# Running sum in fp32r, a shorter streamed router, and the position product moved from VectorE to GpSimd

## The reference

```python
h = _L0_tok_ref(x, W, b)             # path signature of depth 4, then a linear map
h = h + _L0_attn_ref(_layernorm(h), ...)
h = h + _L0_ffn_ref(_layernorm(h), ...)
h = h + _L1_attn_ref(_layernorm(h), ...)   # 8 heads of 16, relative positions
h = h + _L1_ffn_ref(_layernorm(h), ...)    # 64 experts, top 2, 256 places each
# fourth stage
attn1 = einsum('bhqd,bhkd->bhqk', rq, rk)
attn2 = einsum('bhqd,qkd->bhqk', rq, rel_k[idx])
attn = softmax((attn1 + attn2) / sqrt(c))
out = einsum('bhqk,bhkd->bhqd', attn, rv) + einsum('bhqk,qkd->bhqd', attn, rel_v[idx])
# router of the fifth
scores = sigmoid(xf @ gate_w.T); top_scores, top_idx = top_k(scores, 2)
top_scores = top_scores / (top_scores.sum(-1) + 1e-20) * 2.5
pos = cumulative count of the token's expert in the order of tokens - 1
buf[e, pos] = x of the pair, dropped where pos >= 256
```

## Time and profile before

| | us |
|---|---|
| median of 3 runs | 2156.07 (2155.49 to 2164.38) |
| the profiled execution, its own time | 2159.81 |
| its span | 2158.0 |
| signature stage | 0 to 568 |
| second and third stage | 568 to 984 |
| fourth stage, head | 984 to 1023 |
| fourth stage, batches | 1023 to 1811 |
| drain of the router | 1811 to 1888 |
| fifth stage and end | 1888 to 2158 |

### The profile page before, as it was taken

The page is one execution under the profiler, slowest core; times in us unless marked ns, Lnnn a source line. Parts: engine busy times, 40 slices in busy tenths (PEclk is TensorE's granted clock), DMA queues, the critical chain, the costliest instruction groups (busy, mean ns, idle before and its releaser), DMA issues. The chain is left out here.

```text
span 2158.0 us, 59101 instructions
## 1 busy us (share of the span) xinstructions
PE 1747.0 (81%) x21991; PEld 1432.7 (66%) x21991; DVE 1411.1 (65%) x3365; ACT 926.8 (43%) x2288; POOL 848.8 (39%) x1748
## 2 busy tenths in 40 slices
PE   5999999999789739943999999999998996066660
PEld 4888888888577639942887777777777775033440
DVE  6777777777578746655677777777777775123334
ACT  2111111111376407732677666666666663022220
POOL 3333333333016556631012433434444445655551
PEclk9999999999899859975999999999999998588875
DMA  8900000000300012230233333333333332064427
GB/s 309 103 0 0 0 0 0 0 0 0 135 28 26 26 52 70 72 107 25 53 62 71 69 66 67 71 67 70 72 74 76 71 69 45 33 191 123 125 66 242
DMA packets 312522, 147.59 MB, mean 68 GB/s; under 512 B 205094, under 2 KB 291140, under 8 KB 311876
## 3 DMA queue, kind: packets, MB, share of 16 engines
q1 hardware_dynamic: 299732, 118.38, 23.8%
q0 software_dynamic: 12544, 25.91, 3.7%
HBM read 72.03 MB, written 73.37 MB: 67 GB/s over the span
## 5 line engine op out<-in xcount | busy, mean ns | idle before, releaser
L1808 ACT ACTIVATE rel_e<-rel_s_ps,rel_neg_max 128x255 f32<-128x255 f32 x512 | 199.9, 476 | 68.9 <-DVE rel_neg_max L2082 68.4
L495 PE MATMUL tok_main_ps<-tok_w_h,tok_feat_h 128*128 128x512 f32 x512 | 205.6, 402 | 0.9 <-DVE tok_feat_low L99 0.9
L495 PE MATMUL tok_main_ps<-tok_w_h,tok_feat_l 128*128 128x512 f32 x512 | 200.1, 391 | 0.0
L495 PE MATMUL tok_main_ps<-tok_w_l,tok_feat_h 128*128 128x512 f32 x512 | 199.7, 390 | 0.0
L2082 DVE TENSOR_REDUCE rel_neg_max<-rel_s_ps 128x4 f32<-128x1020 f32 x128 | 155.4, 1215 | 51.6 <-PE rel_s_ps L1597 50.0
L2053 DVE SCALAR_TENSOR_TENSOR rel_q_head_l<-rel_qT,all_k_mask,rel_q_head_h 32x256 fp32r<-32x256 f32 x256 | 112.3, 475 | 94.3 <-ACT rel_q_head_h L1799 92.0
L1616 PEld LDWEIGHTS rel_t_ps<-all_k_ident,rel_e 128*128 128x128 f32 x1024 | 110.6, 142 | 83.6 <-issue 80.0
L1616 PE MATMUL rel_t_ps<-all_k_ident,rel_e 128*128 128x128 f32 x1024 | 140.1, 280 | 29.4 <-DVE rel_work L2171 16.2
L84 POOL TENSOR_TENSOR tok_q_pre<-tok_v_q,tok_v 128x128 f32 (+1 forms) x32 | 39.2, 1225 | 312.3 <-DVE tok_q L269 298.0
L1583 PE MATMUL rel_s_ps<-rel_k_h,rel_q_head_h 128*128 128x256 f32 x512 | 155.9, 304 | 4.8 <-DVE rel_q_pos L2063 4.8
L296 DVE TENSOR_REDUCE tok_inc<-tok_prod 128x128 f32<-128x1024 f32 x64 | 128.8, 2012 | 34.9 <-PE tok_small_ps L511 33.8
(11 more groups left out here) (333 smaller groups left out, 4737.0 us busy)
## 6 DMA issues: line engine op xcount, KB each, us to landing
rel_q_rep<-q_rows SPq DMA_DIRECT2D x256, 64.0 KB
o_rows<-rel_rv SPq DMA_DIRECT2D x256, 64.0 KB
x_slots<-early_zeros SPq DMA_DIRECT2D x16, 520.0 KB, 6.5
exp_x<-x_slots SPq DMA_DIRECT2D x32, 260.0 KB, 2.9
y_rows<-early_zeros SPq DMA_DIRECT2D x16, 512.0 KB, 6.5
final_y<-y_rows SPq DMA_DIRECT2D x16, 512.0 KB, 10.1
exp_x<-x_slots SPq DMA_DIRECT2D x72, 65.0 KB, 1.8
rows_y<-y_rows SPq DMA_DIRECT2D x8, 512.0 KB, 6.5
```

The lines of the kernel that those rows point to most:

```text
L495: nc.tensor.matmul(main_ps[s][:, cols], feat[fk][:, s, j, :], w_p[wk][:, j, cols], start=(j == 0 and (fk, wk) == (0, 0)), stop=False)
L1808: last = nc.scalar.activation(e[u % 2][:, n, 0:L], s_ps[u % 2][:, n, 0:L], ACT.Exp, bias=neg_max[u % 2][:, n:n + 1])
```

## The change

In the signature stage the increments are rounded to fp32r by ScalarE (increments) and their remainder is taken by VectorE (increment_remainder); running_sum is four fp32r matmuls on 256, 256, 128 and 128 columns. VectorE's reduction waits for the rounding, not for the sum.

In the fourth stage position_queries goes from VectorE's slot 1 to GpSimd, three batches ahead of GpSimd's loop index, ahead of factors; position_scores waits for it, not content. read_x goes from VectorE's slot 0 to slot 2 and three batches ahead; the query remainders of pairs 0 and then 1 to 3 are taken in slot 3 and the next slot 0 (before: 0 in slot 2, 1 in slot 3, 2 and 3 in slot 0). The router has shorter delays: rows in slot 1 two batches behind, the turn of x1 in slot 3, logits in slot 1 of the next batch, read by VectorE straight from PSUM; count and weigh in slot 1, choose_first, places and scores in slot 2, choose_second and accumulate in slot 3. The scores are all made on VectorE. TensorE's wait for VectorE's copy in slot 1 and the router's matmuls come ahead of project_k.

```diff
@@ signature_tokens
+                def increment_remainder(b):
+                    dve.wait_ge(inc_round, b + 1)
+                    rest(nc.vector, inc_p[1][:], inc[:], inc_p[0][:]).then_inc(inc_rest, 1)
...
+                def increments(b):
+
+                    act.wait_ge(inc_ready, 2 * b + 2)
+                    if not isinstance(b, int) or b >= 1:
+                        act.wait_ge(h_ready, b)
+                    nc.scalar.activation(inc_p[0][:], inc[:], ACT.Copy).then_inc(inc_round, 1)
...
-                    nc.tensor.matmul(h_ps[:, 0, :], upto[:, 0:P], inc[:, 0, :], start=True, stop=True)
-                    nc.tensor.matmul(h_ps[:, 1, :], upto[:, P:T], inc[:, 0, :], start=True, stop=False)
-                    nc.tensor.matmul(h_ps[:, 1, :], upto[:, 0:P], inc[:, 1, :], start=False,
-                                     stop=True).then_inc(h_ready, 1)
+                    both = h_ps.rearrange("p s d -> p (s d)")
+                    for k in range(2):
+                        nc.tensor.matmul(both, upto_r[:, 0:P], inc_p[k][:].rearrange("p s d -> p (s d)"), start=(k == 0),
+                                         stop=False)
+                    for k in range(2):
+                        last = nc.tensor.matmul(h_ps[:, 1, :], upto_r[:, P:T], inc_p[k][:, 0, :], start=False,
+                                                stop=(k == 1))
+                    last.then_inc(h_ready, 1)
@@ relative_attention
-LAG_X, LAG_TOP, LAG_COUNT, LAG_PLACE = 3, 4, 6, 7
+LAG_X, LAG_TOP, LAG_CHOOSE, LAG_COUNT = 2, 3, 4, 5
...
@@ tensor: turn_e, route, slot
-                    if u == 2 and b >= LAG_X:
-                        pe.wait_ge(route_read, b - LAG_X + 1)
-                    if u == 0 and chunk_at(b - 1, LAG_COUNT) is not None:
-                        pe.wait_ge(work_ready, chunk_at(b - 1, LAG_COUNT) + 1)
+                    if u == 0 and b > LAG_X:
+                        pe.wait_ge(route_read, b - LAG_X)
+                    if u == 2 and b >= LAG_TOP:
+                        pe.wait_ge(top_ready, b - LAG_TOP + 1)
+                    if u == 2 and chunk_at(b, LAG_COUNT) is not None:
+                        pe.wait_ge(work_ready, chunk_at(b, LAG_COUNT) + 1)
...
+                    if u == 1:
+                        if chunk_at(bb, LAG_COUNT) is not None:
+                            pe.wait_ge(route_read, min(bb - LAG_X, B))
+                            count(chunk_at(bb, LAG_COUNT))
+                        if LAG_TOP <= bb < B + LAG_TOP:
+                            logits(bb - LAG_TOP)
+                    if u == 3 and LAG_X <= bb < B + LAG_X:
+                        turn_x1(bb - LAG_X)
...
-                    if u == 1 and have(b + 2):
-                        project_k(b + 2)
+                    if u == 1:
+                        pe.wait_ge(eT_v, NU * b + u + 1)
+                        route(b, u)
+                        if have(b + 2):
+                            project_k(b + 2)
@@ scalar
-                    if u == 0 and LAG_X <= bb < B + LAG_X:
+                    if u == 1 and LAG_X <= bb < B + LAG_X:
                         rows(bb - LAG_X)
...
-                    if u == 1:
+                    if u == 3:
                         route(b, u)
...
                     if u % 2 == 0:
                         read_rv(b, u)
+                    if u == 1:
+                        route(b, u)
@@ gpsimd
+                def position_queries(b, r):
+
+                    pool.wait_ge(q_in, 16 * 2 * QUAD * (b + 1))
+                    if after(b, 2):
+                        pool.wait_ge(s_done, NU * (b - 1))
+                    nc.gpsimd.tensor_tensor(
+                        q_pos[r][:], q_rep[:].rearrange("p h (g i) -> p g h i", i=QUAD),
+                        mask4[:].unsqueeze(1).unsqueeze(1).to_broadcast([P, T // (2 * QUAD), H, QUAD]),
+                        ALU.mult).then_inc(qp_ready, 1)
...
+                for b in range(B):
+                    q = chunk_at(b, LAG_CHOOSE)
+                    if q is not None:
+                        locate(q)
+                    if have(b + 3):
+                        position_queries(b + 3, (b + 3) % 2)
+                    factors(b)
+                    if q is not None:
+                        send(q)
@@ vector
-                        if have(b + 2):
-                            read_x(b + 2)
                         if have(b + 1) and after(b, 1):
-                            queries_remainder(b + 1, 1 - r, (2, 3))
+                            queries_remainder(b + 1, 1 - r, (1, 2, 3))
...
                             combine(b - 1, 1)
-                        if have(b + 1) and after(b, 1):
-                            position_queries(b + 1, 1 - r)
...
-                        if have(b + 2):
-                            queries_remainder(b + 2, r, (0,))
+                        if have(b + 3):
+                            read_x(b + 3)
...
                         if have(b + 2):
-                            queries_remainder(b + 2, r, (1,))
-                    route(b, u)
+                            queries_remainder(b + 2, r, (0,))
+                    if u >= 2:
+                        route(b, u)
```

More of the change, by code:

```diff
@@ L1544, in _ @@
                 turn_rows(B - 1, 1)
-                for b in range(B - LAG_X, B):
+                for b in range(B - LAG_X - 1, B):
                     keep_turned(b)
@@ L1921, in tail @@
                     read_n(B - 1, 1)
-                    for bb in range(B, B + LAG_PLACE + 1):
+                    for bb in range(B, B + LAG_COUNT):
                         for u in range(NU):
@@ L2273, in head @@
                             read_v(0, 0)
[L2274 to L2275 removed]
+                    read_x(2)
                     maxima(0, 0)
```

184 lines of the change are left out of this document (82 added, 102 removed).

## The result

The changed kernel takes 2135.3 us and the kernel before 2159.03 beside it, each the median of 8 executions. One execution of each lies far outside the others (3026.13 and 5737.76 us); without them the medians are 2131.92 (2123.97 to 2144.52) and 2157.95. The ratio, without them, is 0.988, 95% interval 0.9846 to 0.9913: 1.2% faster. That is inside the range (2095 to 2150), on the forecast's side; the forecast was 2119.6, so it is 12 us above it, or 16 by the median of all 8. The profiled execution of the changed kernel is nearly the fastest of its runs: 2124.31 us, span 2122.5. For the profiled execution the prediction's sum was 2123.3.

The account below looks back on a forecast made before the run. Bounds: TensorE's work in the signature stage, its waits in attention, GpSimd's queue in the drain. -3.5 - 7 - 4 - 22 = -36.5 on the profiled 2159.8 gives 2123.3; less 3.7 for the median, 2119.6 us; range 2095 to 2150.

Parts of the forecast that it names:

- Signature stage, -3.5: Running sum in four fp32r matmuls, 0.54 us instead of 0.67 in 32 batches, +0.5 at the end: -3.5 us.
- Head, -7: Attention stage's start: VectorE no longer waits for the second q_rep, first scores start earlier: -7 us, or -3.
- Steady batches, -4: Attention batches: 0.34 us gained in each of 22 full batches, about 4 lost at both ends: -4, between -20 and +20.
- Its slots without a collision: Steady batch before any contention: slots 0 and 1 12.33, slot 2 5.9, slot 3 6.0, sum 24.2 us.
- Its collision: GpSimd's product runs across the start of VectorE's three remainders: 0.6 us a batch on slot 0's chain, making 24.8.
- The 25.14 us of before: Length of one batch in the kernel before, read from a two-batch repeat of 50.28 us in TensorE's timeline.
- Slot 2, 5.9: ScalarE's normalised rows move behind read_k and delay read_rv: slot 2 takes 5.9 us instead of 5.27.
- Drain, -22: After the batches, the VectorE-GpSimd-VectorE chain for scores goes and GpSimd is one chunk further: -22 us, bounds -18 and -25.
- Rival 1: The product does not collide with the remainders: 24.2 us a batch, steady -20 instead of -4, 2104 us; chance 0.2.
- Rivals 2 and 4: GpSimd's queue becomes the loop: by contention, 2140 us, chance 0.15; by a product at a third the pace, 2187, 0.05.
- Rival 3: Drain shorter only by its handoffs, 8 us, as something else holds the last chunk: 2133 us; chance 0.1.
- The price of 1.97 us for the product: GpSimd's position product, taken from its nearest traced row, 128x1024 with broadcast operands: 1.97 us, against 1.22 on VectorE.

Follow-up runs that it names:

- e3: Changed kernel with the position product back on VectorE at the end of its slot 1, one batch ahead; 2109.92 us, ratio 0.9788.
- e1: Changed kernel with slot 1's key projection ahead of the wait for eT and made three times over; 2107.98 us, ratio 0.9785.
- e5: Changed kernel unchanged, run again on a chip with stalls; 2262.58 us, ratio 0.9903.
- e10: Changed kernel, position products on VectorE except batches 0 and 1, key projection before eT's wait, ScalarE's rows earlier in slot 1; 2217.1 us, ratio 0.9699.
- e12: The kernel of e10 once more, on a chip without the stalls; 2076.73 us, ratio 0.9631.
- e7: The kernel of e6, with GpSimd's product also waiting for VectorE's last remainder of its batch; 2280.83 us, ratio 0.9974.
- e4: Kernel before with the signature part alone: rounded increments, running sum in four fp32r matmuls; 2153.65 us, ratio 0.9987.
- e6: Changed kernel with GpSimd's product behind the factors of the batch instead of ahead of them; 2276.35 us, ratio 0.996.
- e11: Changed kernel with GpSimd's product made twice; 2381.25 us in one run, beside 2284.55 for the kernel before.

## Why the prediction was right, and where it was not

**The sum.** Over the profiled executions it is -35.5 against -36.5. That is nearer than the terms deserve: the steady batches came out 10.1 us worse than forecast and all other stretches together 9.1 better, 4.4 of it in a stage that the prediction left out.

**Signature stage, -3.5: mis-sized.** The term was 0.54 us for the running sum; it took 0.46. The 128-column fp32r matmuls start 0.06 and 0.11 us before the next instruction, not 0.15. The stage gives 5.8 us (4.4 to 6.5 over the profiles).

**Head, -7: right.** 8.2 us, and e3 shows that all of it is the move of the product: with the product on VectorE the head is as long as before. The first maxima begin at 1001.95; 1013 less the 10.2 us by which the stage begins earlier is 1002.8.

**Steady batches, -4: the step that failed.** They cost 6.1 us more, +4.4 in batches 0 to 5 (predicted +4 for the ends), +1.1 in batches 6 to 28 and +0.6 in the last three. Its slots without a collision were right: 24.2 forecast, 24.24 measured in e3. Its collision was right in size: 0.6 forecast, (128.3 - 112.2) / 29 = 0.55 measured, 0.64 in batches 6 to 28. But that is an average of batches at 0 and at up to 1.64, because a remainder is held until the product ends, and the product starts 1.3 to 3.9 us into the batch where the prediction had 2 to 3. Two things were not right:
- The price of a wait was taken as its length. The sum has slots 0 and 1 longer by the later copy and the 0.6 of the collision, and no term for what TensorE does behind a wait. It idles there for 0.9 us without the collision (e3) and for 1.5 on average with it, and in nine batches (1.56 to 2.53 us) its clock fell. That costs 1.7 us each time. Over the 23 batches 6 to 28 it is 9 x 1.7 / 23 = 0.67 a batch, and 24.24 + 0.64 + 0.67 = 25.55 against 25.46 measured. e1 shows it: the same collision, work in the gap, no fall of the clock.
- The 25.14 us of before were two quiet batches. Over batches 6 to 28 it takes 25.41: there was 0.27 a batch more to gain than the prediction saw, and none of it was gained.

**The median, 12 us above the forecast.** The profiled execution is 1.0 us above its sum. The forecast for the median took off 3.7 more, since the kernel before was profiled in an execution above its median; the changed kernel was profiled in one 7.6 below. The seven executions reach from 2123.97 to 2144.52 us, their mean granted clocks from 0.918 to 0.907, the longer ones mostly at the lower clock. From the profiled execution (0.918) to the slowest (0.907) the time at the lower level goes from 2 x 0.082 x 2122.5 = 348 us to 2 x 0.093 x 2142.7 = 399, which would cost about 25 us; 20 were measured. That fits more long slots in the other executions, but the fastest one has a clock of 0.912, which the same sum would make some 13 us slower than the profiled one. So the cause of the spread is not shown: only one execution on such a chip has a profile, and e5, which was to show it, met the stalls (it has two such slots, in place of nine).

**Slot 2, 5.9: right,** 5.73, and e10 and e12 give its price back by moving ScalarE's rows.

**Drain, -22: right.** From the last slot to the last send it takes 53.3 us instead of 76.0. The last issue ends 51.6 us behind batch 30's statistics, 51.8 forecast:

```profile
1795.89 0.29 DVE L2145 BATCH_NORM_STATS2 all_stats<-all_h 128x6 f32<-128x128 f32 x1
...
1846.82 0.95 POOL L2032 DMA_INDIRECT x_slots<-rel_x,rel_at  x1 [0.31 <-issue]
```

**Rivals.** Rival 1 (no collision) fell for the changed kernel and is what e3, e7 and e12 make true. Rivals 2 and 4 (GpSimd's queue) fell: in the changed kernel ScalarE waits for rel_shift in one batch (0.62 us, batch 30), and with the product doubled in none. Rival 3 fell with the drain. The price of 1.97 us for the product was good: 1.90 in the mean of 32.

**The second and third stage, 0: missed** by 4.4 us, with a clock that on chips of this kind goes with the new attention stage's code (e4) and has no cause shown.

The Trainium skill, GPSIMD Engine Reference, Key points, says that the two engines contend for SBUF where an instruction has two SBUF inputs; the trace agrees: six two-input remainders take 3.87 instead of 2.69 us beside a product of 1.90. The advice of the Trainium skill, GPSIMD Engine Reference, Elementwise, side-by-side cycle accounting, to keep elementwise work on VectorE agrees with e3 for full batches, not for the head, where VectorE was what everything waited for.

## What to carry to other kernels

Price a new wait on TensorE by its length and by what follows it: here waits from 1.56 us on were at times followed by 3.4 us at half speed. Fill a gap with work that has to be done anyway (here the key projection) before trying to shorten what causes it. An engine that takes over work to relieve another should be looked at in time, not in sum: GpSimd's product was free in itself and cost 1.2 us a batch, clock included, through the neighbour that it ran beside. Look at single instructions there and not only at a group's mean, since one of them may hold all of the loss. A move pays where the old engine was late (the head), and may be made for that stretch alone. Read slot lengths over all batches, before as well as after, not from one quiet pair.

## What the runs showed of the hardware

- TensorE's granted clock fell after waits of 1.56 to 2.53 us inside a stream that was otherwise dense, and matmuls ran at half speed for some 3.4 us, which cost 1.7 us each time. It is not the length alone: waits in a slot 1 of 2.02 us (changed kernel, batch 25), of 2.26 (several batches of e6) and of 2.85 (e11, batch 11) left it at 1.00, one of 1.56 (changed kernel, batch 24) did not. What else decides is open.
- More matmuls made the kernel faster: e1 does two key projections of 0.43 us more per batch, with all three ahead of the wait, and takes 21 us less between the profiled executions.
- A 128x1024 product on GpSimd takes 1.90 us and holds one of VectorE's 32x256 remainders, which have two inputs in SBUF, until 0.28 us behind its own end: 0.47 us become up to 2.1, and the six take up to 4.33 instead of 2.69. The remainders behind it keep their time. GpSimd's own small operations take 0.31 to 0.44 us beside them instead of 0.19 to 0.24.
- On two of four chips TensorE's stream stopped, with no semaphore that the profile shows, for 0.2 to 1.4 us at a time or some 5 us at once while GpSimd issued indirect sends, and the kernel before took 2285 and 2288 us instead of 2156 and 2158. Orders between versions shift with it: without a send e7's odd batches take 24.3 us, as e5's do, and e7's ratio is still 0.997 where e5's is 0.990. So versions should be compared on the same chip and their profiles checked for such slots.
